# Scores three key tiles ahead of the values, and a new order around them, in a float32 attention block

## The chip, the cores and the metric

The kernel runs on one core of a Trainium2 chip. The metric is the device time of one execution in microseconds. Three runs were timed, and one more execution was profiled.

## The reference

Two residual blocks over `x` of shape (4, 1024, 1024) in float32, cut to what matters:

```python
# block 0
adj = emb_s * emb_t * softmax(x) / sqrt(n)          # diagonal set to -inf
x = x + (1.0 where adj is among the 10240 largest of its 1024 x 1024, else 0)
# block 1: 16 heads of 64
scale, shift = split(cond @ W_emb + b_emb)
xn = rms_norm(x, g_norm) * (1 + scale) + shift
q, k, v = heads(xn @ W_qkv)
q, k = rms_norm(q, g_q), rms_norm(k, g_k)
o = softmax(q @ k.T * d ** -0.5) @ v
x = x + o + o @ W_out
```

## The kernel before

The kernel is written engine by engine: five classes (`Sync`, `Pool`, `Scalar`, `Vector`, `Tensor`) each emit their engine's instructions in a fixed order, and semaphores join them. There is no scheduler; an engine does what comes next in its list, or waits.

Each of the four batches is a loop over eight pairs of heads (`pair`, one method in each class), followed by a `boundary` that projects the outputs and normalises the next batch's features. In a pair `gp` two kinds of work are woven together on TensorE (line 1575 on):

- The attention of pair `gp`. For each head `hh` and each of eight key tiles (128 keys, 1024 queries): `scores` (L1524, four matmuls of 512 columns into two of the four `pst` banks), `exp` on ScalarE (L858 writes the rounded `ph`, L864 the full `pf`), `low` on Pool (L530, `pl = pf - ph`), and `values` (L1544 with `ph` against the values' high and low parts, L1550 with `pl`; accumulated in `ppv`). Over both heads these are 16 tiles, counted `w` within the pair.
- The preparation of pair `gp + 1`, for seven of the eight pairs (`prep`). For each of eight token tiles: `prep_tile` (L1467, three groups of eight matmuls of 384 columns: features high x weights high, high x low, low x high), then ScalarE takes squares, the values' high part and q and k out of `pax` (L825, L828, L835), DVE sums the squares (L1208), scales the sums (L1211) and makes the values' low part (`value_low`, L1218), Pool builds the stacked rows in `stage` (L618 to L636), TensorE transposes them (`transpose_tile`, L1485), and ScalarE copies them out (`stack_tile`, L842 to L844). When all eight are there, `score_max` (L1504, 16 tiles of two matmuls) gives the products of which DVE takes the row maxima (`row_max`, L1225).

Four rules of order matter for the change.

The buffers `ph`, `pf` and `pl` are threefold, so `exp` of tile `w` waits until the values of tile `w - 3` are done. `pst` holds two tiles, so `scores` of tile `w` waits for the exponentials of tile `w - 2`:

```python
e.wait_ge(t_pv, CST + w - 2)      # exp, L856
e.wait_ge(t_ex, CST + w - 1)      # scores, L1521
```

`pax` holds one tile of a preparation, so `prep_tile` of tile `t` waits for the values' low part of tile `t - 1` (semaphore `a_v`). `score_max` of a tile writes the two halves of the other `pax` use, and each half waits for the reduction of the same half of the tile before.

The outputs of pair `gp - 1` are turned at the start of pair `gp`: `out_tokens` (L1560) and `out_rows` (L1572) on TensorE, in two halves, each copied by ScalarE into `ostg` (L877). The transposes of the first prepared tile use the same bank and wait for both copies (`t_oe`).

SyncE issues all DMAs in program order. In a pair it loads the low features of token tiles 0 and 1 (`load_xl`, L348, 512 KB each), then waits for each copied half of the outputs and stores it (L458), and only then loads the low features of tiles 2 to 7. TensorE waits for such a load at the third group of `prep_tile`:

```python
if prep:
    for t in range(2):
        self.load_xl(gp + 1, t)
if not first:
    for h in range(2):
        e.wait_ge(t_oe, 2 * (gp - 1) + h + 1)
        e.dma_start(oT_pairs[...], ostg[...])
if prep:
    for t in range(2, T):
        self.load_xl(gp + 1, t)
```

Beside this, in batches 0 to 2, a search over the next batch's keys for the 10240th largest value runs on DVE in all pairs: counting passes (L1004), and every second tile an update (`search_update`, L1011 to L1016) behind a sum by TensorE (L1477) and a copy by ScalarE (L816). In batch 0, five of the pairs that follow the first, and the first itself, also split the weights of a later pair into high and low parts (L705 on ScalarE, L523 on Pool).

The slots: in steps 8 to 15 the table `slots` says which `score_max` tiles stand before the values, inside them (before their last matmul) and behind them.

Of the kernel before, what the change touches and what calls it, by code (L numbers as in the profile page):

```python
# [48 lines left out]
def cond_block(nc, x, s_in, cond, w_emb, b_emb, g_norm, w_qkv, g_q, g_k, w_out, out, ctx):  # L49
    B, N, D = x.shape  # L50
    T = N // P
# [48 lines left out]
    ahead = sb("ahead", [P, 2, 3], I32)  # L100
# [385 lines left out]
    class Pool:  # L486
# [156 lines left out]
        def pair(self, b, i, par, search, prep, first):  # L643
            e, gp = self.e, PAIRS * b + i
# [26 lines left out]
            for t in range(2, T):  # L671
                if prep:
                    self.prep_tile(gp + 1, t, 1 - par, False)
                self.low(gp, (t + 1) // T, (t + 1) % T)
# [11 lines left out]
    class Scalar:  # L686
# [192 lines left out]
        def pair(self, b, i, par, search, prep, first):  # L879
# [15 lines left out]
            self.exp(gp, 0, 2, new)  # L895
            if not first:
                self.out_rows(gp - 1, 1)
            if prep:
                self.prep_tile(gp + 1, 1 - par, 1)
            self.exp(gp, 0, 3)  # L900
# [4 lines left out]
            for t in range(2, T - 1):  # L905
                if prep:
                    self.prep_tile(gp + 1, 1 - par, t + 1, z=before[t + 1])
                    if t < T - 2:
                        self.stack_tile(gp + 1, 1 - par, t)
                self.exp(gp, (t + 2) // T, (t + 2) % T)  # L910
                if search and not prep and t == 2:
                    self.search_tot(z)
            if prep:
                self.stack_tile(gp + 1, 1 - par, T - 2)
# [5 lines left out]
            self.exp(gp, 1, 1)  # L920
# [18 lines left out]
    class Vector:  # L939
# [304 lines left out]
        def pair(self, b, i, par, search, prep, first):  # L1244
# [11 lines left out]
            for t in range(T):  # L1256
                if prep:
                    self.prep_sums(gp + 1, t)
                if t > 0 and before[t] is not None:
                    self.search_update(before[t])  # L1260
                if prep:
                    self.value_low(gp + 1, 1 - par, t)
# [18 lines left out]
    class Tensor:  # L1281
# [293 lines left out]
        def pair(self, b, i, par, search, prep, first):  # L1575
# [4 lines left out]
            def fill(what):  # L1580
# [3 lines left out]
                elif what is not None:  # L1584
                    self.score_max(gp + 1, 1 - par, what)

            slots = {8: [None, 0, 1], 9: [2, 3, None], 10: [4, 5, None], 11: [6, 7, None], 12: [8, 9, None],
                     13: [10, 11, None], 14: [12, 13, "row"], 15: [14, 15, None]} if prep else {}
# [24 lines left out]
            for t in range(2 * T):  # L1613
                gap = slots.get(t, [None] * 3)
                if t + 2 < 2 * T and not (prep and t == 1):
                    self.scores(gp, par, (t + 2) // T, (t + 2) % T)
# [4 lines left out]
                if prep and t == 0:  # L1621
                    self.prep_tile(gp + 1, 1)
                    self.scores(gp, par, 0, 3)
# [5 lines left out]
                if prep and t == 1:  # L1629
                    self.transpose_tile(gp + 1, 1)  # L1630
                if prep and 1 <= t <= T - 3:
                    self.prep_tile(gp + 1, t + 2, z=before[t + 2])
                    self.transpose_tile(gp + 1, t + 1)
# [74 lines left out]
```

## Time and profile before

| | |
|---|---|
| median of 3 runs | 3757.48 us |
| lowest and highest run | 3756.02 and 3767.08 us |
| the profiled execution | 3765.85 us, of which the profile's span is 3763.9 us |
| TensorE (PE) busy | 3484.9 us, 93% of the span |
| DVE busy | 2480.7 us, 66% |
| ScalarE (ACT) busy | 2027.0 us, 54% |
| Pool busy | 2480.0 us, 66% |
| mean granted TensorE clock | 0.973 of full |

PE stands for TensorE's matmuls, PEld for its weight loads, SPq for SyncE's queue of DMA issues. In rows of the timeline the columns are: start, duration, engine, line, operation, output and inputs by the program's names, shapes, and how many instructions were merged; in brackets the idle time ahead of the row and what ended it. Matmuls overlap by some 0.17 us and their ends are modelled, so the distance from start to start is the better measure. A granted clock of 1.00 is the 2.4 GHz level, 0.50 the 1.2 GHz level. Two views of waits are used: who waited for whom, with the idle time summed, the number of waits and the longest; and the busy time of every engine in a given stretch.

### The profile page before, as it was taken

The numbers are of one execution on the slowest core, as the hardware profiler recorded it, in microseconds if no ns is written. First come the engines' busy times: TensorE is split into PE (matmuls) and PEld (weight loads), VectorE is DVE, ScalarE is ACT, GpSimd is POOL, SyncE is SP. The second block draws the span as 40 slices with busy tenths as digits, with TensorE's granted clock in tenths as the row PEclk, the third lists the DMA queues.
The fourth block names the chain that finished last, engine by engine and source line by source line (L and its number), as shares of the span: only waits on it lengthen the run. The fifth ranks groups of instructions, "written<-read, shape, count | busy, mean of one in ns | idle before, by whom it ended". The sixth has DMA issues, their size and how long they took to land.

```text
span 3763.9 us, 46982 instructions
## 1 busy us (share of the span) xinstructions
PE 3484.9 (93%) x16661; PEld 2542.8 (68%) x16672; DVE 2480.7 (66%) x4056; ACT 2027.0 (54%) x3331; POOL 2480.0 (66%) x2583
## 2 busy tenths in 40 slices
PE   4847999999999999999999999999999999999999
PEld 1225777777756677777756677777755677777754
DVE  8995777777787777777787677777777333333321
ACT  4635555555546355655545455555554455555650
POOL 2027778777646677777756677777765577777750
PEclk9966999999999999999999999999999999999999
DMA  7033223232245222222237222222235322222222
GB/s 291 1 101 112 93 98 105 99 105 101 95 154 193 95 87 99 102 96 84 73 111 235 90 85 89 85 85 88 101 110 172 112 88 87 90 84 91 77 86 94
DMA packets 163305, 399.51 MB, mean 106 GB/s; under 512 B 11848, under 2 KB 83584, under 8 KB 153216
## 3 DMA queue, kind: packets, MB, share of 16 engines
q1 hardware_dynamic: 163072, 396.52, 29.8%
q8 instruction: 133, 2.18, 0.2%
q14 instruction: 100, 0.82, 0.1%
HBM read 302.10 MB, written 94.37 MB: 105 GB/s over the span
## 4 chain that ended last, share of the span: by engine, by line
PE 69%; DVE 13%; POOL 10%; ACT 4%; DMA 2%; issue 2%; SPq 0%; POOLq 0%; DVEq 0%; ACTq 0%
PE pax L1467 26%; PE pst L1524 9%; PE ppv L1544 9%; PE pst L1440 8%; PE pax L1504 5%; PE ppv L1550 4%; POOL pl L530 3%; DVE mx L1225 3%; PE pst L1304 2%; PE pax L1485 2%; DMA xl<-xl_scr 2%; POOL xlo L554 1%; DVE xr L1056 1%; POOL wl L523 1%; POOL rs L618 1%
## 5 line engine op out<-in xcount | busy, mean ns | idle before, releaser
L530 POOL TENSOR_TENSOR pl<-pf,ph 128x1024 fp32r<-128x1024 f32 x512 | 1219.6, 2392 | 203.1 <-ACT pf L864 200.8
L1004 DVE TENSOR_SCALAR_CACHE_REDUCE trash<-keys,state 128x2048 uint8<-128x2048 f32 x384 | 899.2, 2342 | 7.7
L1225 DVE TENSOR_REDUCE mx<-pax 128x1 f32<-128x512 f32 x960 | 618.2, 686 | 271.2 <-PE pax L1504 270.5
L858 ACT ACTIVATE ph<-pst 128x1024 fp32r<-128x1024 f32 x512 | 523.1, 1022 | 223.3 <-PE pst L1524 215.5
L864 ACT ACTIVATE pf<-pst 128x1024 f32<-128x1024 f32 x512 | 522.7, 1021 | 0.4 <-DMA out_x<-pf 0.4
L1208 DVE TENSOR_REDUCE ss<-sq 128x4 f32<-128x256 f32 x256 | 107.3, 419 | 609.3 <-ACT sq L825 609.3
L618 POOL TENSOR_TENSOR rs<-rs,half 128x4 f32<-128x4 f32 x256 | 265.2, 1036 | 292.9 <-DVE rs L1211 288.9
L1467 PE MATMUL pax<-wh,xh 128*128 128x384 f32 x1920 | 394.2, 348 | 46.1 <-DVE vl L1218 39.8
L1467 PEld LDWEIGHTS pax<-wh,xh 128*128 128x128 f32 x1920 | 339.0, 192 | 81.4 <-DVE vl L1218 55.7
L1467 PE MATMUL pax<-wl,xh 128*128 128x384 f32 x1920 | 385.1, 339 | 0.0
L1504 PE MATMUL pax<-sA 65*128 65x512 f32 x960 | 351.7, 433 | 33.8 <-DVE mx L1225 17.5
L1550 PE MATMUL ppv<-pl,vh 128*65 128x512 f32 x1024 | 360.1, 397 | 7.9 <-POOL pl L530 7.9
L1467 PE MATMUL pax<-wh,xl 128*128 128x384 f32 x1792 | 356.5, 342 | 10.6 <-DMA xl<-xl_scr 10.6
L1524 PE MATMUL pst<-sA 65*128 65x512 f32 x1024 | 343.5, 417 | 5.0 <-ACT sA L849 4.4
L1467 PEld LDWEIGHTS pax<-wl,xh 128*128 128x128 f32 x1920 | 338.6, 190 | 0.0
L1467 PEld LDWEIGHTS pax<-wh,xl 128*128 128x128 f32 x1792 | 321.1, 190 | 12.6 <-DMA xl<-xl_scr 12.6
L825 ACT ACTIVATE sq<-pax 128x256 f32<-128x256 f32 x240 | 91.2, 380 | 437.5 <-PE pax L1467 437.3
L1524 PE MATMUL pst<-sB 128*128 128x512 f32 x1024 | 326.0, 400 | 0.0
L1544 PE MATMUL ppv<-ph,vh 128*65 128x512 f32 x1024 | 322.0, 396 | 0.9 <-issue 0.5
L1544 PE MATMUL ppv<-ph,vl 128*65 128x512 f32 x1024 | 319.9, 393 | 0.0
L1504 PEld LDWEIGHTS pax<-sA 65*128 65x128 f32 x960 | 179.9, 190 | 177.9 <-DVE mx L1225 131.6
L546 POOL TENSOR_SCALAR rsx<-ssx 128x1 f32<-128x1 f32 x32 | 22.6, 706 | 325.6 <-ACT otok L728 324.3
(198 smaller groups left out, 5625.7 us busy)
## 6 DMA issues: line engine op xcount, KB each, us to landing
xl<-xl_scr SPq DMA_DIRECT2D x224, 512.0 KB, 3.3
wh<-w_scr SPq DMA_DIRECT2D x24, 1536.0 KB, 6.2
wl<-w_scr SPq DMA_DIRECT2D x24, 1536.0 KB, 9.6
keys<-in_x SPq DMA_DIRECT2D x32, 512.0 KB, 5.3
xl_scr<-xlo SPq DMA_DIRECT2D x64, 256.0 KB, 3.2
wo<-wo_scr SPq DMA_DIRECT2D x4, 4096.0 KB, 13.6
pf<-out_x SPq DMA_DIRECT2D x64, 256.0 KB, 3.8
out_x<-pf SPq DMA_DIRECT2D x64, 256.0 KB, 3.1
```

Source lines behind the costliest of these rows:

```text
L530: e.tensor_tensor(pl[:, w % 3, :], pf[:, w % 3, :], ph[:, w % 3, :].bitcast(F32), ALU.subtract).then_inc(t_lo, 1)
L618: e.tensor_tensor(rs[:, cols], rs[:, cols], half4[:], ALU.pow).then_inc(a_rs, 1)
L858: e.activation(ph[:, w % 3, :], src, ACT.Exp, scale=DH ** -0.5).then_inc(t_eh, 1)
L864: e.activation(pf[:, w % 3, :], src, ACT.Exp, scale=DH ** -0.5).then_inc(t_ex, 1)
L1004: e.tensor_scalar(trash[:], kv, thr_f, None, ALU.is_ge, ALU.add, accum_out=cnt[:, c:c + 1]).then_inc(z_cnt, 1)
L1225: e.tensor_reduce(mx2[:, j // T, j % T, c:c + 1], max_banks(alone, j)[:, c, :], axis=AX, op=ALU.max).then_inc(m_mx, 1)
L1440: i = e.matmul(pst[:, q % 4, :], heads_of(b, k, t), wo[b % 2][:, k, c * HALF:(c + 1) * HALF], start=(k == 0), stop=(k == KT - 1), skip_gro ...
L1467: i = e.matmul(qkv_bank(alone, t)[:, 0:6 * DH], a, w[:, k, :, :].rearrange("p s c -> p (s c)"), start=(n == 0), stop=(n == 3 * KT - 1), sk ...
L1504: e.matmul(max_banks(alone, j)[:, c, :], sA[par][0:DH + 1, hh, qt * P:(qt + 1) * P], sA[par][0:DH + 1, 2 + hh, c * HALF:(c + 1) * HALF], s ...
L1524: i = e.matmul(pst[:, 2 * (kt % 2) + c, :], op[0:k, 2 + hh, kt * P:(kt + 1) * P], op[0:k, hh, c * HALF:(c + 1) * HALF], start=(m == 0), st ...
L1544: e.matmul(ppv[0:DH + 1, c, :], v[:, par, kt, hh, :], ph[:, w % 3, c * HALF:(c + 1) * HALF], start=(kt == 0 and m == 0), stop=False, skip_ ...
L1550: i = e.matmul(ppv[0:DH + 1, c, :], vh[:, par, kt, hh, :], pl[:, w % 3, c * HALF:(c + 1) * HALF], start=False, stop=(kt == T - 1), skip_gr ...
```

## The change

On TensorE, in pairs with preparation: the scores run three tiles ahead of the values instead of two; in step 0 the preparation of tile 1 and the scores of tile 3 stand ahead of the values of tile 0; in steps 1 to 6 the transposes of tile `t` and then the scores of tile `t + 3` stand ahead of the values; the slots of the score maxima are dealt out anew. On ScalarE the exponentials of a step stand ahead of that step's copies, and in step 0 the copy of the second half of the output rows stands behind the exponentials of tile 3. On Pool the low part stands ahead of a tile's stage. On DVE the values' low part stands ahead of the search update. Last pairs of a batch, without preparation, keep their order. SyncE's order is unchanged.

```diff
@@ Pool.pair
             for t in range(2, T):
+                self.low(gp, (t + 1) // T, (t + 1) % T)
                 if prep:
                     self.prep_tile(gp + 1, t, 1 - par, False)
-                self.low(gp, (t + 1) // T, (t + 1) % T)
@@ Scalar.pair
             self.exp(gp, 0, 2, new)
+            if prep:
+                self.prep_tile(gp + 1, 1 - par, 1)
+                self.exp(gp, 0, 3)
             if not first:
                 self.out_rows(gp - 1, 1)
-            if prep:
-                self.prep_tile(gp + 1, 1 - par, 1)
-            self.exp(gp, 0, 3)
+            if not prep:
+                self.exp(gp, 0, 3)
...
             for t in range(2, T - 1):
+                self.exp(gp, (t + 2) // T, (t + 2) % T)
                 if prep:
                     self.prep_tile(gp + 1, 1 - par, t + 1, z=before[t + 1])
-                    if t < T - 2:
-                        self.stack_tile(gp + 1, 1 - par, t)
-                self.exp(gp, (t + 2) // T, (t + 2) % T)
+                    self.stack_tile(gp + 1, 1 - par, t)
...
             if prep:
-                self.stack_tile(gp + 1, 1 - par, T - 2)
+                self.exp(gp, 1, 1)
             self.out_move(gp, 0, (PAIRS - 1) * b + i)
...
             if prep:
                 self.stack_tile(gp + 1, 1 - par, T - 1)
-            self.exp(gp, 1, 1)
+            else:
+                self.exp(gp, 1, 1)
@@ Vector.pair
                 if prep:
                     self.prep_sums(gp + 1, t)
+                if prep:
+                    self.value_low(gp + 1, 1 - par, t)
                 if t > 0 and before[t] is not None:
                     self.search_update(before[t])
-                if prep:
-                    self.value_low(gp + 1, 1 - par, t)
@@ Tensor.pair
-            slots = {8: [None, 0, 1], 9: [2, 3, None], 10: [4, 5, None], 11: [6, 7, None], 12: [8, 9, None],
-                     13: [10, 11, None], 14: [12, 13, "row"], 15: [14, 15, None]} if prep else {}
+            slots = {8: [None, 0, 1], 9: [2, 3, None], 10: [4, 5, 6], 11: [7, 8, None], 12: [9, 10, None],
+                     13: [11, 12, None], 14: [13, 14, "row"], 15: [15, None, None]} if prep else {}
+            ahead = 3 if prep else 2
...
             for t in range(2 * T):
                 gap = slots.get(t, [None] * 3)
-                if t + 2 < 2 * T and not (prep and t == 1):
-                    self.scores(gp, par, (t + 2) // T, (t + 2) % T)
+                if prep and t == 0:
+                    self.scores(gp, par, 0, 2)
+                    self.prep_tile(gp + 1, 1)
+                if prep and 0 < t < T - 1:
+                    self.transpose_tile(gp + 1, t)
+                if t + ahead < 2 * T:
+                    self.scores(gp, par, (t + ahead) // T, (t + ahead) % T)
                 fill(gap[0])
                 self.values(gp, par, t // T, t % T, lambda: fill(gap[1]))
                 if t == 0 and not first:
                     self.out_rows(gp - 1, 1)
                 if prep and t == 0:
-                    self.prep_tile(gp + 1, 1)
-                    self.scores(gp, par, 0, 3)
                     self.prep_tile(gp + 1, 2, hi=8)
...
-                if prep and t == 1:
-                    self.transpose_tile(gp + 1, 1)
                 if prep and 1 <= t <= T - 3:
                     self.prep_tile(gp + 1, t + 2, z=before[t + 2])
-                    self.transpose_tile(gp + 1, t + 1)
```

TensorE at the start of a pair with outputs to write, before, from the scores of tile 2 (`pst<-sA`, `pst<-sB`) to the first group of the preparation of tile 2 (`otok` are the output rows, `wh,xh` begins a preparation):

```order
L1524 MATMUL pst<-sA 128x512 x2
L1524 MATMUL pst<-sB 128x512 x2
L1544 MATMUL ppv<-ph,vh 65x512 x2
L1544 MATMUL ppv<-ph,vl 65x512 x2
L1550 MATMUL ppv<-pl,vh 65x512 x2
L1572 MATMUL pax<-identr,otok 128x128 x4
L1467 MATMUL pax<-wh,xh 128x384 x8
L1467 MATMUL pax<-wl,xh 128x384 x8
L1467 MATMUL pax<-wh,xl 128x384 x8
```

The same place after the change, as far as the first group of the preparation of tile 2:

```order
L1526 MATMUL pst<-sA 128x512 x2
L1526 MATMUL pst<-sB 128x512 x2
L1469 MATMUL pax<-wh,xh 128x384 x8
L1469 MATMUL pax<-wl,xh 128x384 x8
L1469 MATMUL pax<-wh,xl 128x384 x8
L1526 MATMUL pst<-sA 128x512 x2
L1526 MATMUL pst<-sB 128x512 x2
L1546 MATMUL ppv<-ph,vh 65x512 x2
L1546 MATMUL ppv<-ph,vl 65x512 x2
L1552 MATMUL ppv<-pl,vh 65x512 x2
L1574 MATMUL pax<-identr,otok 128x128 x4
L1469 MATMUL pax<-wh,xh 128x384 x8
```

The values of tile 0 and the output rows behind them have moved behind a whole preparation and the scores of tile 3. (Lines are two higher in the changed file.)

ScalarE at the same place, before, from the first half of the output rows (`ostg`) to the exponentials of tile 3:

```order
L877 ACTIVATE ostg<-pax 128x512
L858 ACTIVATE ph<-pst 128x1024
L864 ACTIVATE pf<-pst 128x1024
L877 ACTIVATE ostg<-pax 128x512
L825 ACTIVATE sq<-pax 128x256
L828 ACTIVATE vh<-pax 128x2x64
L835 ACTIVATE qkn<-pax 128x256
L858 ACTIVATE ph<-pst 128x1024
L864 ACTIVATE pf<-pst 128x1024
```

And after:

```order
L877 ACTIVATE ostg<-pax 128x512
L858 ACTIVATE ph<-pst 128x1024
L864 ACTIVATE pf<-pst 128x1024
L825 ACTIVATE sq<-pax 128x256
L828 ACTIVATE vh<-pax 128x2x64
L835 ACTIVATE qkn<-pax 128x256
L858 ACTIVATE ph<-pst 128x1024
L864 ACTIVATE pf<-pst 128x1024
L877 ACTIVATE ostg<-pax 128x512
```

The second copy of output rows has moved behind the copies of preparation 1 and the exponentials of tile 3.

TensorE in step 10, after the change, from score maximum 4 (`pax<-sA`) to the scores of the next step:

```order
L1506 MATMUL pax<-sA 128x512 x2
L1546 MATMUL ppv<-ph,vh 65x512 x2
L1546 MATMUL ppv<-ph,vl 65x512 x2
L1552 MATMUL ppv<-pl,vh 65x512
L1506 MATMUL pax<-sA 128x512 x2
L1552 MATMUL ppv<-pl,vh 65x512
L1506 MATMUL pax<-sA 128x512 x2
L1526 MATMUL pst<-sA 128x512 x2
```

Before, the last `pax<-sA` row of these wasn't there; the scores followed the one matmul on `pl` at once.

## Rows read from the trace of the kernel before

**Rows 1.** Busy time by stretch, of three pairs: us, engines' busy (instructions), clock, DMA.

```profile
core 0: us, PE busy (x) PEld busy (x) DVE busy (x) ACT busy (x) POOL busy (x), PEclk, DMA share, GB/s
752.50:845.60 93.10, 88.16 (x465) 69.73 (x465) 69.03 (x112) 55.33 (x98) 74.47 (x77) 1.00 0.30 102
1444.10:1534.40 90.30, 87.48 (x465) 69.92 (x465) 69.06 (x112) 52.64 (x95) 67.54 (x74) 1.00 0.24 88
3158.00:3246.60 88.60, 86.44 (x457) 69.03 (x457) 29.97 (x64) 51.98 (x87) 67.49 (x74) 1.00 0.24 90
```

**Rows 2.** Waits of PE, 1444 to 1534 us (three rows) and 3158 to 3246 us (last).

```profile
PE pax L1467 <- DVE vl L1218: 1.5, 2, 0.9
PE pax L1504 <- DVE mx L1225: 0.6, 2, 0.3
PE pax L1485 <- POOL stage L636: 0.2, 1, 0.2
...
PE pax L1467 <- DVE vl L1218: 0.9, 1, 0.9
```

**Rows 3.** Timeline of PE, 1451 to 1468 us.

```profile
1452.45 0.63 PE L1544 MATMUL ppv<-ph,vh 128*65 128x512 f32 x2
...
1453.83 0.60 PE L1572 MATMUL pax<-identr,otok 128*128 128x128 f32 x4
...
1454.19 1.64 PE L1467 MATMUL pax<-wh,xh 128*128 128x384 f32 x8
...
1458.46 0.64 PE L1524 MATMUL pst<-sA 65*128 65x512 f32 x2
...
1460.43 1.66 PE L1467 MATMUL pax<-wh,xh 128*128 128x384 f32 x8 [0.87 <-DVE vl L1218]
...
1463.69 1.57 PE L1467 MATMUL pax<-wh,xl 128*128 128x384 f32 x8
...
1466.73 0.46 PE L1485 MATMUL pax<-identr,stage 128*128 128x128 f32 x4
...
1467.83 1.66 PE L1467 MATMUL pax<-wh,xh 128*128 128x384 f32 x8 [0.64 <-DVE vl L1218]
```

**Rows 4.** Timeline of ACT, exponentials 2, second output rows, exponentials 3.

```profile
1454.48 1.06 ACT L864 ACTIVATE pf<-pst 128x1024 f32<-128x1024 f32 x1
...
1455.38 0.65 ACT L877 ACTIVATE ostg<-pax 128x512 f32<-128x512 f32 x1
...
1459.60 1.02 ACT L858 ACTIVATE ph<-pst 128x1024 fp32r<-128x1024 f32 x1
...
1460.52 1.03 ACT L864 ACTIVATE pf<-pst 128x1024 f32<-128x1024 f32 x1
```

**Rows 5.** SyncE's issues, then landings of L348: tile 2 alone, and 1450 to 1475.

```profile
1453.73 2.64 SPq L458 DMA_DIRECT2D oT_scr<-ostg  x2
1456.41 16.23 SPq L348 DMA_DIRECT2D xl<-xl_scr  x4
...
DMA to landing us min/median/max: 3.7/3.7/3.7
...
DMA to landing us min/median/max: 3.2/3.5/4.3
```

**Rows 6.** Timeline of POOL and DVE, 1455 to 1464 us.

```profile
1455.42 4.74 POOL L530 TENSOR_TENSOR pl<-pf,ph 128x1024 fp32r<-128x1024 f32 x2
...
1459.61 0.58 DVE L1211 TENSOR_SCALAR rs<-ss 128x4 f32<-128x4 f32 x1
...
1460.30 2.33 DVE L1004 TENSOR_SCALAR_CACHE_REDUCE trash<-keys,state 128x2048 uint8<-128x2048 f32 x1
...
1463.73 0.46 POOL L636 TENSOR_TENSOR stage<-qkn,stage 128x128 fp32r<-128x128 f32 x1
...
1466.66 0.17 DVE L1211 TENSOR_SCALAR rs<-ss 128x4 f32<-128x4 f32 x1
```

**Rows 7.** Timeline of PE and DVE at score maxima 0 and 1.

```profile
1508.05 0.63 PE L1504 MATMUL pax<-sA 65*128 65x512 f32 x2
1508.51 0.40 PE L1550 MATMUL ppv<-pl,vh 128*65 128x512 f32 x1
1509.22 1.10 PE L1504 MATMUL pax<-sA 65*128 65x512 f32 x2 [0.31 <-DVE mx L1225]
1510.16 0.62 PE L1524 MATMUL pst<-sA 65*128 65x512 f32 x2
...
1508.47 2.57 DVE L1225 TENSOR_REDUCE mx<-pax 128x1 f32<-128x512 f32 x4 [2.28 <-PE pax L1504]
```

**Rows 8.** First pair of batch 1: PE's wait, and 3.4 us behind it.

```profile
PE pax L1467 <- DVE vl L1218: 2.4, 2, 1.8
...
1279.00:1282.40 3.40, 3.40 (x15) 3.30 (x14) 3.36 (x3) 0.99 (x3) 2.20 (x6) 0.50 0.00 0
```

**Rows 9.** Waits of PE, a pair of batch 0, 752 to 845 us.

```profile
PE pax L1467 <- DMA xl<-xl_scr: 1.7, 1, 1.7
...
PE ppv L1550 <- POOL pl L530: 0.5, 2, 0.2
```

**Rows 10.** The 3.4 us behind two waits for a load, batch 0.

```profile
571.40:574.80 3.40, 3.40 (x19) 3.09 (x20) 1.26 (x4) 1.69 (x4) 0.59 (x1) 1.00 0.14 52
...
664.60:668.00 3.40, 3.40 (x10) 3.30 (x11) 0.07 (x1) 0.49 (x3) 0.00 (x0) 0.50 0.14 52
```

## The prediction, made before the changed kernel had run

> **What bounds the kernel.** I cut the trace into pairs first. A pair of heads that also prepares the next pair takes 93.1 us in batch 0, 90.3 in batches 1 and 2, 88.6 in batch 3, TensorE is busy for all but 2 to 5 us of it, and its granted clock is 1.00 [rows 1]. There are 28 such pairs, seven in each batch, and the change touches them alone. So TensorE's own order bounds them, and only what lengthens or shortens its waits counts. I measure a wait from the start of one group to the start of the next, less what the group takes elsewhere, since the ends of matmuls are modelled.
>
> The waits of one pair, by who ended them, are in [rows 2]: two on the low part of the values, two on the row maxima, one on Pool's stage. The timeline [rows 3] places the first two. Scores of tile 3 start at 1458.46 and take 0.93, but the preparation of tile 2 starts at 1460.43: 1.0 us lost. The preparation of tile 3 starts at 1467.83, 1.1 after four transposes that take 0.3: 0.8 lost. Batch 3 has the first alone (last row) [rows 2].
>
> **The change, part by part.** One preparation is 4.2 us, one scores group 0.93, one values group 1.4 (1452.45 to 1453.83, with its output rows 0.36 more) [rows 3]. No work is added; order decides everything.
>
> *Second wait.* Scores of tile 4 now stand between the preparations of tiles 2 and 3, 0.93 us of cover against a wait of 0.8, and the value's low part no longer stands behind the search update. It goes: -0.8 in the 18 pairs with search that are not a batch's first, **-14**. What is late next there is Pool's stage of tile 1, ready at 1464.2 (1463.73 + 0.46) [rows 6], some 2 us before it is asked for.
>
> *Output rows and what hangs on them.* This is the part that the words of the change don't name. Values 0 move behind preparation 1 and scores 3; ScalarE now does exponentials 3 ahead of the second half of the output rows. Exponentials of tile w wait for values w - 3, because they reuse the buffer. So on the old clock: preparation 1 starts at 1452.45 instead of 1454.19, ends 1456.65; scores 3 to 1457.6; values 0 to 1458.95, drained at 1459.15. Exponentials 3 take 1.95 (1459.60 to 1461.55) [rows 4]: to 1461.1. The copy of the output rows ends 0.5 after the exponential ahead of it (1455.54 and 1456.03) [rows 4]: at 1461.6. The old time was 1456.03. Behind this copy wait, in SyncE's queue, the second store of the rows and then the load of the low features for tile 2 [rows 5]: it was issued 0.4 after the copy and landed 3.7 later. Now it is issued at 1462.0 and lands at 1465.7. TensorE needs it for the third group of preparation 2, which started at 1463.69 [rows 3]. By then the same matmuls have been issued in both orders, so the difference is the whole cost: **+2.0 us**. The first wait (1.0) and the transposes of tile 0, which wait for the same copy, lie inside that path and cost nothing on top. The 24 pairs that have output rows to write: 24 x 2.0 = **+48**. Bounds: the load may land in 3.2 or 4.3 (the shortest and longest of the four around there [rows 5]), so 1.5 to 2.6 each.
>
> *Score maxima.* Scores now end one step earlier, and the table of slots puts maximum 6 right behind 5, and 11 right behind 10, with one 0.24 us matmul between. The trace shows such a neighbourhood: maximum 0 starts at 1508.05, and with maximum 1 the two take to 1510.16, 2.11 us, where their five matmuls need 0.46 + 0.24 + 0.46 = 1.16. The price is 0.95, for DVE needs 2.57 for four reductions [rows 7]. Before, this happens at 0-1 and 11-12 in full, and at 13-14 with the output of the row maxima between (0.46). After, the full ones are 0-1, 5-6, 10-11 and 12-13, and 14-15 has the rows between. Two more: 2 x 0.95 x 28 = **+53**. Bounds: DVE is idle for part of each step, so a later one could be cheaper, 0.5; more than 0.95 it can't be without an earlier debt, which the scores between pay off.
>
> *First pair of a batch.* It has no output rows, so the +2.0 is absent. Its two waits show 2.4 us idle, the longer 1.8 [rows 8], and after the longer one the granted clock is 0.50 for 3.4 us. Afterwards Pool's stage for tile 1 (second subtraction, then 4 us) is the latest and keeps about 1 us. Gain 3 each, four pairs: **-12**.
>
> *Batch 0.* Pool also splits weights in five of these pairs, works without a break at the end and makes values wait; the low-feature load of tile 0 comes 1.7 late behind it [rows 9]. With exponentials a step earlier Pool starts this row of work some 2 us earlier: about -1 each, **-5**; the ends are 0 and -2.
>
> *Clock.* The new wait for the load leaves TensorE idle for about 2 us in one piece. The trace has two waits on such a load of 1.7 us idle each, almost alike: after the one that ended at 571.3 the granted clock stayed 1.00, with 19 matmuls in 3.4 us; after the one that ended at 664.5 it was 0.50 (the 1.2 GHz level) with 10 in 3.4 us [rows 10]. Nine of nineteen lost is 1.6 us. Which of the two a pair meets the trace doesn't tell; I take half of 24: 12 x 1.6 = **+19**, ends 0 and +38.
>
> *Update behind the low part.* The search's small DVE operations come 0.3 later, and the counting passes behind them (2.33 each [rows 6], two a step) fill 4.7 of the 7 us of a step (4.2 + 0.93 + 1.4 and the transposes); nobody waits for them: 0.
>
> *Steps 3 to 7.* ScalarE, Pool and TensorE keep their spacing (Pool has 2.4 for a subtraction and 4 for a stage, 6.4 us of work in 7.0); 0, and the 0.3 on Pool's last stage stays.
>
> **Sum:** 48 - 14 + 53 - 12 - 5 + 19 = **+89**. It is made on the profiled execution of 3765.85 us (span 3763.9), which is 8.4 above the median of the three runs, 3757.48. The waits are the same in both, so I put the 89 on the median: **3846**.
>
> **A rule beside a row.** The small scaling of the squares' sums on DVE takes 0.17 as a rule, and 0.58 at 1459.61, where it ends at 1460.19, within 0.03 of Pool's second subtraction (1455.42 + 4.74) [rows 6]. So the first wait comes from Pool holding DVE, and moving values behind the preparation doesn't by itself end it: the scaling would now be issued at about 1457.8, inside the same two subtractions. It matters for the second rival below. The Trainium skill, GPSIMD Engine Reference, section Specifications, says that GpSimd shares its SBUF interfaces with VectorE, with contention for VectorE instructions in a two-port mode or with two SBUF inputs; by that rule the first wait stays wherever the long subtractions lie beside the scaling, and the trace agrees. By it the second rival comes out at 3779 and not at 3755.
>
> **The rivals.**
> 1. *The forecast*, 0.64: both new waits. Its own range: no clock loss at all, short landings and cheaper maxima give 3757 + 36 - 14 + 28 - 12 - 5 = 3790; all clocks lost, long landings and nothing gained in batch 0 give 3757 + 62 - 14 + 53 - 12 + 38 = 3884.
> 2. *The load isn't late, only the maxima cost*, 0.16. It needs the copy of the output rows before about 1459.6, that is exponentials 3 not held by values 0. Against it speaks the wait in the code. The first wait stays as it is, since Pool holds DVE in the same way. 53 - 14 - 12 - 5 = +22: 3779. Were the first wait to vanish too, 24 less, 3755, no difference.
> 3. *Faster*, 0.09. Mechanism: the extra neighbours among the maxima are free, because DVE has only 32 reductions of 0.64 us (21 us) for the 25 us that the maxima take, and the load is in time. The old waits then go: 28 x 1.0 + 21 x 0.8, with the first pairs' clock (4 x 1.6) and batch 0's 5: -56, 3701. It decides at the step from maximum 5 to 6: if it takes 1.16 rather than 2.11 us. Against it: the reductions can't begin before their maximum is there, as at 0-1.
> 4. *No net change*, 0.05: maxima at half price and the load late by less than its cover.
> 5. *More than the range*, 0.06: a debt that grows through steps 3 to 7, such as Pool's stage late at every tile, 0.5 us in six steps of 28 pairs, +84 more: 3930.
>
> A measurement of this kernel can tell about 0.3% (11 us) from no change. Slower by more: 0.86, cases 1, 2 and 5. Same: 0.05. Faster: 0.09. The range has to leave out no more than 0.2: I take 3775 to 3878, which holds the forecast without its last corner, and case 2.
>
> **What would show it.** Right: in a pair with output rows TensorE waits for the load of low features some 2 us at tile 2; that load is issued at about 18 us from the pair's first output transposes instead of 12.3; four full stalls of 0.95 among the maxima instead of two; the pairs of batches 1 and 2 take 93 to 95 us instead of 90.3, those of batch 3 some 92.5 to 94; the wait at tile 3 is gone; short stretches at clock 0.50. Wrong: pairs at 92 us with no wait on the load (case 2), or below 90 (case 3).

## The result and the profile after

| | before | after |
|---|---|---|
| median, 6 runs each on the same chips | 3763.35 us | 3873.16 us (3862.23 to 3876.79) |
| ratio | | 1.029, 95% interval 1.027 to 1.031 |
| the profiled execution | 3765.85 us, span 3763.9 | 3874.18 us, span 3872.3 |
| TensorE (PE) busy | 3484.9 us | 3537.6 us |
| mean granted clock | 0.973 | 0.964 |

The changed kernel is slower by 110 us (3873.16 - 3763.35); 89 had been forecast. In the changed file TensorE's and DVE's lines are two higher than before.

Waits of PE over the whole span of the changed kernel (who waited for whom: us in total, times, longest):

```profile
PE pax L1469 <- DMA xl<-xl_scr: 62.5, 24, 3.6
...
PE pax L1506 <- DVE mx L1227: 34.8, 112, 0.3
PE pax L1487 <- POOL stage L636: 28.0, 42, 4.5
PE pax L1469 <- DVE vl L1220: 19.3, 23, 0.9
```

The same view of the kernel before:

```profile
PE pax L1467 <- DVE vl L1218: 39.8, 49, 1.8
...
PE pax L1485 <- POOL stage L636: 24.4, 37, 4.5
...
PE pax L1504 <- DVE mx L1225: 17.5, 56, 0.3
PE pax L1467 <- DMA xl<-xl_scr: 10.6, 6, 2.1
```

Three lines moved most. The low-feature load, formerly waited for in 6 places, is waited for in 24: the pairs with output rows to write. The maxima stall 4 times a pair instead of 2 (112 and 56 over 28 pairs). The value's low part is waited for 23 times instead of 49. What remains there is the first wait. Pool's stage is waited for a little longer, 28.0 us instead of 24.4.

A pair whose clock stayed at 1.00, and the 3.4 us behind two of the new waits (us, busy by engine, clock, DMA):

```profile
2253.60:2347.80 94.20, 88.48 (x465) 70.21 (x465) 70.86 (x112) 53.02 (x95) 67.50 (x74) 1.00 0.23 84
...
2276.10:2279.50 3.40, 3.40 (x20) 3.04 (x21) 0.84 (x4) 1.51 (x7) 0.18 (x1) 1.00 0.30 95
1480.10:1483.50 3.40, 2.93 (x10) 2.93 (x11) 0.00 (x0) 0.00 (x0) 0.07 (x1) 0.50 0.02 10
```

The pair takes 94.2 us where [rows 1] had 90.3; other pairs of batches 1 and 2 run to 99.0, and the difference is mostly the clock. The last line shows it: it begins 0.47 us before its wait ends, at 1480.57, and its 10 matmuls run in the 2.93 us behind that, at clock 0.50. From here on, time at clock 0.50 is added up over the 24 pairs that have output rows to write, each from its first output transpose to that of the pair behind it: 13.7 us before, all of it in batch 0, and 105.8 in the changed kernel. I now go through this pair, which starts at 2253.6. TensorE:

```profile
2267.09 0.63 PE L1546 MATMUL ppv<-ph,vh 128*65 128x512 f32 x2
...
2269.93 1.66 PE L1469 MATMUL pax<-wh,xh 128*128 128x384 f32 x8 [0.86 <-DVE vl L1220]
2271.43 0.46 PE L1487 MATMUL pax<-identr,stage 128*128 128x128 f32 x4
2271.72 1.63 PE L1469 MATMUL pax<-wl,xh 128*128 128x384 f32 x8
2276.09 1.68 PE L1469 MATMUL pax<-wh,xl 128*128 128x384 f32 x8 [2.74 <-DMA xl<-xl_scr]
...
2280.50 0.69 PE L1469 MATMUL pax<-wh,xh 128*128 128x384 f32 x3
```

The third group of preparation 2 starts 22.5 us into the pair; in [rows 3] it started at 19.6 (1463.69 - 1444.10). So 2.9 us are lost; over all 24 pairs the group starts 2.8 later in the mean, if 19.6 is taken for batch 0 too. Preparation 3 starts at 2280.50, with no bracket: the second wait has gone. ScalarE and SyncE's queue show what the load hung on:

```profile
2268.74 1.02 ACT L858 ACTIVATE ph<-pst 128x1024 fp32r<-128x1024 f32 x1 [1.56 <-PE ppv L1552]
2269.66 1.02 ACT L864 ACTIVATE pf<-pst 128x1024 f32<-128x1024 f32 x1
2270.56 0.61 ACT L877 ACTIVATE ostg<-pax 128x512 f32<-128x512 f32 x1
...
2263.23 8.28 SPq L458 DMA_DIRECT2D oT_scr<-ostg  x2
2271.55 6.57 SPq L348 DMA_DIRECT2D xl<-xl_scr  x3
```

Exponentials 3 wait for values 0, the copy of the rows stands behind them, and the load leaves at 2271.55, 17.95 into the pair (12.3 before, [rows 5]). It landed 4.5 us later.

### The profile page after: what moved, and what is told of

The parts are those of the page before. It is cut to its first block, busy times and chain, and to the rows that moved or that the text cites. A ratio compares the mean times of both kernels' runs of the same rounds, so it can differ in the third digit from the quotient of the medians.

```text
span 3872.3 us, 46982 instructions
## 1 busy us (share of the span) xinstructions
PE 3537.6 (91%) x16661; PEld 2577.6 (67%) x16672; DVE 2522.6 (65%) x4056; ACT 2038.1 (53%) x3331; POOL 2478.7 (64%) x2583
## 4 chain that ended last, share of the span: by engine, by line
PE 68%; DVE 12%; POOL 9%; ACT 4%; DMA 3%; issue 2%; SPq 0%; POOLq 0%; DVEq 0%; ACTq 0%
PE pax L1469 23%; PE ppv L1546 10%; PE pst L1526 10%; PE pst L1442 7%; DVE mx L1227 5%; PE pax L1506 5%; PE ppv L1552 4%; DMA xl<-xl_scr 3%; PE pst L1306 2%; PE pax L1487 2%; POOL xlo L554 2%; POOL rs L618 1%; DVE xr L1058 1%; POOL pl L530 1%; POOL qkn L621 1%
## 5 line engine op out<-in xcount | busy, mean ns | idle before, releaser
L1469 PE MATMUL pax<-wh,xl 128*128 128x384 f32 x1792 | 370.6, 351 | 62.5 <-DMA xl<-xl_scr 62.5
L1506 PE MATMUL pax<-sA 65*128 65x512 f32 x960 | 370.3, 443 | 56.6 <-DVE mx L1227 34.8
L1469 PEld LDWEIGHTS pax<-wh,xh 128*128 128x128 f32 x1920 | 348.2, 194 | 58.9 <-DVE vl L1220 24.8
L1469 PEld LDWEIGHTS pax<-wh,xl 128*128 128x128 f32 x1792 | 329.2, 195 | 70.3 <-DMA xl<-xl_scr 70.2
L825 ACT ACTIVATE sq<-pax 128x256 f32<-128x256 f32 x240 | 91.2, 380 | 320.4 <-PE pax L1469 320.2
L1526 PEld LDWEIGHTS pst<-sB 128*128 128x128 f32 x1024 | 199.5, 195 | 46.9
```

Of the source, the lines that this page charges most:

```text
L1469: i = e.matmul(qkv_bank(alone, t)[:, 0:6 * DH], a, w[:, k, :, :].rearrange("p s c -> p (s c)"), start=(n == 0), stop=(n == 3 * KT - 1), sk ...
L1506: e.matmul(max_banks(alone, j)[:, c, :], sA[par][0:DH + 1, hh, qt * P:(qt + 1) * P], sA[par][0:DH + 1, 2 + hh, c * HALF:(c + 1) * HALF], s ...
L1526: i = e.matmul(pst[:, 2 * (kt % 2) + c, :], op[0:k, 2 + hh, kt * P:(kt + 1) * P], op[0:k, hh, c * HALF:(c + 1) * HALF], start=(m == 0), st ...
```

## The experiments

Each was timed beside the kernel before on the same chips (whose medians there are 3763.8 to 3765.8 us); ratios are to that, with the 95% interval.

**The load taken out of its queue place.** SyncE issues the load of tile 2 between the two stores.

```diff
                     e.dma_start(oT_pairs[...], ostg[...])
+                    if prep and h == 0:
+                        self.load_xl(gp + 1, 2)
             if prep:
-                for t in range(2, T):
+                for t in range(2 if first else 3, T):
```

> The changed kernel, but SyncE issues the load of the low features of tile 2 between the two stores of output rows instead of behind both. Theory 1 (the load waits in SyncE's queue behind a copy that waits for values 0): the load is issued about 10 us into a pair and lands before 15, TensorE's wait of about 3 us at the third group of preparation 2 is gone, and with it most of the short stretches at clock 0.50 behind it: 24 x 2.9 = 70 less and 25 to 30 for the clock, so 3770 to 3785. The first wait of 1.0 at preparation 2 stays. Theory 2 (the new order itself, a preparation without values between, is what costs; the load only happens to end it): another wait takes its place at the same group or the transposes ahead of it, and the time stays above 3840.

Measured 3765.14 us, ratio 1.0006 (0.9996 to 1.0015). One DMA in another place takes back 108 of the 110 us. TensorE waits for no load of low features any more, and pairs take 91.2 us in batches 0 to 2 alike. It came out below the expected span because two more things went with the stall: the 105.8 us at clock 0.50 fall to nothing, and batch 0, whose pairs took 93.1 to 94.8 before, waits no more for the load of tile 0.

**The old slots under the new order.** The table of slots put back, the rest as changed.

```diff
-            slots = {8: [None, 0, 1], 9: [2, 3, None], 10: [4, 5, 6], 11: [7, 8, None], ...
+            slots = {8: [None, 0, 1], 9: [2, 3, None], 10: [4, 5, None], 11: [6, 7, None], ...
```

> The changed kernel with the old table of slots for the score maxima (4,5 / 6,7 / ... / 14,15), scores still three ahead. Theory 1: neighbouring maxima cost 0.95 us each; there are three full ones a pair (0-1, 9-10, 11-12) instead of four, so 28 x 0.95 = 27 less: about 3846. Theory 2 (the maxima are free, DVE has time enough): no difference, 3873.

Measured 3856.08 us, 1.025 (1.0232 to 1.0268): 17 less than the changed kernel, where one stall of 0.95 in 28 pairs makes 27. The stalls did fall as they should:

```profile
PE pax L1506 <- DVE mx L1227: 26.3, 84, 0.3
```

84 is three a pair, as expected. The profiled executions differ by 22.7 us (3874.18 and 3851.45), the medians by 17. Of the other 4 to 10 us the trace shows 4: it has 30 waits for the low-feature load instead of 24, and the six more, all for tile 0 in batch 0, come to 4.0 us. The rest isn't settled; both kernels lose an amount to the clock that changes from run to run (four runs of this one lie between 3851.45 and 3861.92).

**Both together.**

> Both: the load of tile 2 between the stores, and the old slots. Theory 1: the two are apart in time and add, 3873 - 97 - 27 = about 3749, somewhat below the kernel before (3763). Theory 2: 3840 or more.

Measured 3743.76 us, 0.9948 (0.9932 to 0.9964). With the load early, the old slots are worth 21 us (3765.14 - 3743.76). So the order of the change, without its late load and one of its two extra stalls, is faster than the kernel before.

**The new slots alone, in the kernel before.**

> The kernel before with the new table of slots alone. Theory 1: neighbours are then 0-1, 5-6 and 12-13 in full, and 14-15 with the rows between; one more than before, 28 x 0.95 = 27 more, about 3790. Theory 2 (maxima free): no difference.

Measured 3787.57 us, 1.0062 (1.0049 to 1.0075). With scores two ahead, the scores still lie between maxima 10 and 11, so one stall is added, not two. The stretch of one pair:

```profile
1445.70:1536.90 91.20, 88.00 (x464) 69.79 (x464) 69.02 (x112) 52.60 (x95) 67.63 (x74) 1.00 0.24 87
```

The waits on the maxima over the whole span, three a pair:

```profile
PE pax L1504 <- DVE mx L1225: 25.5, 84, 0.3
```

A pair takes 91.2 instead of 90.3: 0.92 for one neighbourhood, in the mean of the 18 such pairs of batches 1 to 3, against the 0.95 read off [rows 7]. In batch 0 the pairs grow by 0.3 only, since waits for Pool's low part get shorter beside it.

**The copy of the rows ahead of exponentials 3.** In the changed kernel, on ScalarE.

```diff
             if prep:
                 self.prep_tile(gp + 1, 1 - par, 1)
-                self.exp(gp, 0, 3)
             if not first:
                 self.out_rows(gp - 1, 1)
-            if not prep:
-                self.exp(gp, 0, 3)
+            self.exp(gp, 0, 3)
```

> The changed kernel, but ScalarE copies the second half of the output rows ahead of exponentials 3 (where TensorE has them ready at about 15.4 us into the pair). Theory 1: the copy ends 1.6 us earlier, the load is issued 1.6 earlier, and a wait of about 1.3 instead of 3 us is left at the third group of preparation 2: 24 x 1.6 = 38 less and some of the clock, 3815 to 3835. Theory 2: nothing, or the wait of the exponentials moves elsewhere: above 3860.

Measured 3800.09 us, 1.0093 (1.0077 to 1.0109): 73 less, where 38 and some of the clock were expected, so it fell below the expected span. The wait shrank as it should, by 33 us in all (62.5 to 29.6). What was underrated is the clock: of the 105.8 us at 0.50 only 6.8 are left. Less is saved than by moving the load itself, since the rows are turned behind values 0 and the copy can't come before that. What is left of the wait:

```profile
PE pax L1467 <- DMA xl<-xl_scr: 29.6, 24, 2.9
```

**The landing.** The forecast had the load land in 3.7 us; here it took 4.5, and the load of tile 3 was issued directly behind it. In the changed kernel SyncE now holds that load until tile 2's has landed.

```diff
                 for t in range(2, T):
+                    if t == 3:
+                        e.wait_ge(d_xl[0], 16 * (T * (gp - b) // 2 + 2))
                     self.load_xl(gp + 1, t)
```

> The changed kernel, with SyncE waiting until the load for tile 2 has landed before it issues the one for tile 3. It asks why the wait for the load was 2.9 us longer than the old start of that group and not 2.0. Theory 1: in the changed order the load for tile 3 is ready to go at once behind that for tile 2 and shares the DMA engines with it, so that tile 2 lands in 4.5 (3.8 to 5.3) instead of 3.7; held back, tile 2 lands in 3.7 again, every one of 24 waits is 0.8 shorter, 19 less, and perhaps some of the clock: 3840 to 3855. Theory 2 (the landing is longer for another cause, such as the search's or stores' traffic): the landing stays at 4.5 and the time within 5 of 3873.

Measured 3861.11 us, 1.0259 (1.0243 to 1.0275), 12 less than the changed kernel and 6 above the expected span. In the trace the tile 2 load's median landing over the 24 pairs went from 4.4 (3.7 to 5.3) back to 3.8, and the 24 waits from 2.6 us to 2.1 in the mean, 0.5 each where 0.8 was expected. In the pair that starts at 2241.2 the third group stands 21.65 in:

```profile
2262.85 2.87 PE L1471 MATMUL pax<-wh,xl 128*128 128x384 f32 x8 [1.91 <-DMA xl<-xl_scr]
```

That is 2.05 later than before, against the 2.0 of the forecast; over all 24 pairs it is 2.3 instead of 2.8. So the chain was priced rightly, and most of the rest was the second load close behind. Two pairs still had landings of 4.8 and 5.1 us, which nothing here explains. (Its profiled execution took 3844.84 us, the least of its four, with 54.6 us at clock 0.50.)

**The value's low part ahead of the update, alone.** In the kernel before, on DVE.

```diff
+                if prep:
+                    self.value_low(gp + 1, 1 - par, t)
                 if t > 0 and before[t] is not None:
                     self.search_update(before[t])
-                if prep:
-                    self.value_low(gp + 1, 1 - par, t)
```

> The kernel before with one part of the change alone: on DVE the values' low part stands ahead of the search update. Theory 1: the wait of 0.8 at preparation 3 comes from the update (0.7 us of small operations) that the low part stood behind; it goes in the 21 pairs with search: 21 x 0.7 = 15 less, 0.4%. Theory 2 (the wait belongs to the chain square, sum, low part, which is too long whatever the update does): under 4 less.

Measured 3748.70 us, 0.9959 (0.9946 to 0.9973). It removes the whole second wait. A pair takes 89.6 us:

```profile
1436.10:1525.70 89.60, 87.44 (x464) 69.93 (x464) 69.10 (x113) 52.69 (x95) 67.73 (x74) 1.00 0.25 89
```

And PE's waits for the value's low part in it, one where [rows 2] has two:

```profile
PE pax L1467 <- DVE vl L1218: 0.8, 1, 0.8
```

**Pool's subtraction 2 behind the stage of tile 1, alone.** In the kernel before. This part is not in the change: it tests why the first wait is there.

```diff
             self.low(gp, 0, 1)
-            self.low(gp, 0, 2)
             if prep:
                 self.prep_tile(gp + 1, 1, 1 - par, False)
+            self.low(gp, 0, 2)
```

> The kernel before, but on Pool the low part of exponential tile 2 stands behind the stage of token tile 1 instead of ahead of it, so that no long Pool subtraction runs while DVE wants to scale the squares' sums. Theory 1 (Pool holds DVE): the scaling takes 0.17 and not 0.58 (1.48 in first pairs), the values' low part ends 0.4 earlier, and the wait of 1.0 at preparation 2 shrinks to about 0.6; in first pairs it goes from 1.9 to 0.5 and the stretch at clock 0.50 with it: 24 x 0.4 + 4 x 3 = 22 less. Theory 2 (the length of the scaling is its own): no difference there.

Measured 3743.58 us, 0.9947 (0.9934 to 0.9959). At this place DVE's scaling no longer lies beside a subtraction, and the first wait falls from 1.0 to 0.6 (the scores of tile 3 start at 1451.04 and take 0.93):

```profile
1452.18 0.17 DVE L1211 TENSOR_SCALAR rs<-ss 128x4 f32<-128x4 f32 x1
...
1452.60 1.66 PE L1467 MATMUL pax<-wh,xh 128*128 128x384 f32 x8 [0.46 <-DVE vl L1218]
```

The 24 pairs behind a batch's first give 12 of the profiled execution's 22 us, the stretches from a batch's last pair to the next one's second 11.

**The last two together.**

> The two edits of the kernel before together: the values' low part ahead of the update on DVE, low part 2 behind the stage of tile 1 on Pool. Theory 1: they add, 15 + 22 = 37 less, 3726, faster than both kernels by 1%. Theory 2: under 5 less.

Measured 3730.06 us, 0.9908 (0.9895 to 0.9922). The two are separate: 15.6 and 20.7 alone make 36, and 34 are there.

**Four parts mended in the changed kernel.** Load ahead, old slots, rows before exponentials 3, and Pool's subtraction 2 behind stage 1; the scores stay three ahead.

> The changed kernel with four edits: load of tile 2 between the stores, old slots, output rows ahead of exponentials 3 on ScalarE, and low part 2 behind the stage of tile 1 on Pool. Theory 1: against the kernel with the first two (3744) the first wait of 1.0 goes, since nothing long is on Pool when DVE scales, and the transposes of tile 0 no longer wait for the copy: 24 x 1.0 and a little in first pairs, 3710 to 3722, below the 3730 of the kernel before with two orders changed. Theory 2 (the first wait is a chain of its own length): 3740.

Measured 3743.14 us, 0.9947 (0.9935 to 0.996): a miss by at least 20. The first wait and the load's wait are gone, but there is a new one at tile 3. TensorE, DVE and Pool in the pair that starts at 1423.0:

```profile
1446.74 1.65 PE L1469 MATMUL pax<-wh,xh 128*128 128x384 f32 x8 [0.77 <-DVE vl L1220]
...
1444.39 2.11 DVE L1213 TENSOR_SCALAR rs<-ss 128x4 f32<-128x4 f32 x1
...
1441.73 4.74 POOL L532 TENSOR_TENSOR pl<-pf,ph 128x1024 fp32r<-128x1024 f32 x2
```

The change puts Pool's subtraction 3 ahead of the stage of tile 2. With subtraction 2 moved behind the stage of tile 1 the two adjoin: 4.74 us without a gap, to 1446.47. DVE's scaling of tile 2 is issued into them and ends at 1446.50. The wait has moved one tile on.

**Maxima spread evenly.** The kernel with the last two orders, with each inner maximum ahead of the fourth of the six matmuls of `values`, and the first eight maxima dealt anew.

```diff
                 for c in range(2):
+                    if m and c and between is not None:
+                        between()
...
-            slots = {8: [None, 0, 1], 9: [2, 3, None], 10: [4, 5, None], 11: [6, 7, None], ...
+            slots = {8: [None, None, 0], 9: [1, 2, None], 10: [3, 4, None], 11: [5, 6, 7], ...
```

> The kernel before with the two orders changed (3730), and the maxima dealt out evenly: the one inside the values stands after three of their six matmuls instead of after five, step 8 has one, steps 9 to 15 two, step 11 three. Theory 1 (a neighbour costs because DVE needs 1.3 us for its two reductions and TensorE comes back after 0.7): starts are then never closer than 1.16, about five stalls of 0.13 are left instead of 0.95 + 0.95 + 0.46, 1.7 less in 28 pairs, 48 in all: about 3682. Theory 2 (the price is that of switching between maxima and values): no gain, or a loss, 3730 or more.

Measured 3769.69 us, 1.0012 (1.0003 to 1.0021): 40 above its base, where a gain was expected. PE, then DVE, at three maxima:

```profile
1499.01 0.63 PE L1504 MATMUL pax<-sA 65*128 65x512 f32 x2
1500.19 1.10 PE L1504 MATMUL pax<-sA 65*128 65x512 f32 x2
1501.12 0.40 PE L1546 MATMUL ppv<-ph,vl 128*65 128x512 f32 x1
1501.36 0.63 PE L1550 MATMUL ppv<-pl,vh 128*65 128x512 f32 x2
...
1499.44 2.58 DVE L1225 TENSOR_REDUCE mx<-pax 128x1 f32<-128x512 f32 x4 [0.87 <-PE pax L1504]
```

Three matmuls between two maxima put them 1.18 apart, and the second then takes 0.93 instead of 0.47 (from its start to that of the matmul behind it). Its second half needs the bank that DVE releases 0.43 + 1.29 us after the first maximum's start. With five matmuls between, as in the old slots, they are 1.63 apart and nothing is lost (the changed kernel, 2323.53 and 2325.16; DVE idles 0.32 between them):

```profile
2323.53 0.63 PE L1506 MATMUL pax<-sA 65*128 65x512 f32 x2
...
2325.16 0.66 PE L1506 MATMUL pax<-sA 65*128 65x512 f32 x2
...
2325.59 1.29 DVE L1227 TENSOR_REDUCE mx<-pax 128x1 f32<-128x512 f32 x2 [0.32 <-PE pax L1506]
```

So an even deal made nearly every second maximum stall in order to save the few that did. A new wait came with it: with one maximum less in step 8, the scores behind it wait 0.5 us for the exponentials, 31 waits and 14.0 us in the whole trace, where the kernel before has 3 and 0.6.

**Values 0 behind preparation 1, with the scores two ahead.** The kernel with the last two orders, the load between the stores, and TensorE's step 0 as in the change. On ScalarE the copies of preparation 1 now stand ahead of the second copy of output rows, and exponentials 3 stay behind it. The diff below shows TensorE alone.

```diff
+                if prep and t == 0:
+                    self.prep_tile(gp + 1, 1)
+                    self.scores(gp, par, 0, 3)
                 fill(gap[0])
                 self.values(...)
                 if t == 0 and not first:
                     self.out_rows(gp - 1, 1)
                 if prep and t == 0:
-                    self.prep_tile(gp + 1, 1)
-                    self.scores(gp, par, 0, 3)
                     self.prep_tile(gp + 1, 2, hi=8)
```

> The kernel before, with the two orders that each gained (the update behind v's low part on VectorE, the low features of tile 2 behind the staging of tile 1 on GpSimd, together 3730), the load of tile 2's low features between the two stores, and on TensorE the preparation of tile 1 and the scores of tile 3 ahead of the values of tile 0; the scores stay two key tiles ahead and keep their old slots, ScalarE copies the output rows ahead of the exponentials of tile 3. Theory 1 (what is left of the first wait, 0.62 in each of 24 pairs and more in the first ones, stands only because TensorE comes to the preparation of tile 1 with nothing in front that could be done): about 3714 (3708 to 3720), faster than both kernels, pairs of about 88.5. GpSimd's subtractions for tiles 2 and 3 should not run back to back as they did with four parts changed, so VectorE's scaling isn't held. Theory 2 (a later values 0 makes the output rows and the load late as in the changed kernel, or VectorE is held and a new wait stands at tile 2 or 3): 3730 or more.

Measured 3709.26 us, 0.986 (0.9841 to 0.9879): faster than both kernels, by 55 and by 164 us. TensorE, DVE and Pool at the same place:

```profile
1440.81 0.60 PE L1574 MATMUL pax<-identr,otok 128*128 128x128 f32 x4
1441.17 1.64 PE L1469 MATMUL pax<-wh,xh 128*128 128x384 f32 x8
...
1447.28 0.17 DVE L1213 TENSOR_SCALAR rs<-ss 128x4 f32<-128x4 f32 x1
...
1437.26 2.38 POOL L532 TENSOR_TENSOR pl<-pf,ph 128x1024 fp32r<-128x1024 f32 x1
...
1444.62 2.40 POOL L532 TENSOR_TENSOR pl<-pf,ph 128x1024 fp32r<-128x1024 f32 x1
```

The stretch of this pair:

```profile
1425.90:1514.30 88.40, 87.10 (x465) 70.11 (x465) 68.75 (x112) 52.59 (x95) 67.64 (x74) 1.00 0.25 90
```

Values and output rows fill what was the first wait, Pool's subtractions lie apart, and the pair takes 88.4 us. Of [rows 2] only the maxima (0.6) and Pool's stage (0.2) are left.

## Why the prediction was right, and where its sizes were off

The sign and the mechanism hold: 3873 lies in the range, and the two new waits stand where they were put. It lies 5 us below the range's upper end. Of the 27 us between 3846 and 3873, 6 are the kernel before, whose median was 3757.48 in the three runs that the forecast had and 3763.35 in six. By its own steps, against the difference of the two spans, 108.4 us:

| term | forecast | found | from |
|---|---|---|---|
| second wait | -14 | -14 | gone in the trace; alone -15.6 |
| output rows and the load | +48 | +66 | 24 pairs, 2.8 in the mean |
| score maxima | +53 | +52 | 56 more stalls; 0.92 for each, measured alone |
| first pairs of a batch | -12 | -17 | start of the span to batch 0's second pair, and from each batch's last pair to the next one's second: -1.5, -2.9, -4.6, -0.2, together -9, and the 7 that their own maxima cost are in the line above |
| batch 0 | -5 | -17 | six pairs: shortest 94.3 instead of 93.1 + 4.0 |
| clock | +19 | +38 | what remains of 108.4; not measured by itself |

Load and clock cost 37 us more than forecast, and the first pairs and batch 0 gained 17 more than forecast. That the sum is off by only 19 is in part luck: errors of both signs met in it. (Part of the first pairs' gain is clock too: those stretches have 17 us less at 0.50.)

**Output rows.** The chain was foretold link by link: the load issued 17.9 into the pair (found 17.95), exponentials 3 held by values 0. The step that was mis-sized is "landed 3.7 later". A single load had shown that figure [rows 5]; here it landed in 4.5 (4.4 in the median of the 24 pairs), and tile 3's load was issued right behind it. With that load held back the loss was 2.05 in one pair and 2.3 in the mean. The bound of the forecast, 2.6, was too low, for it was taken from landings around and not from a pair of loads issued together.

**Score maxima.** Right in size and place. The changed kernel alone shows the count of four; the price comes from the slots alone, 0.92 for one more in a pair (+23.3 over all 28, batch 0 giving some of it back).

**Second and first wait.** The second went, and its cause is the update: one exchange on DVE does it without anything else of the change. The first stayed, as forecast, and the row beside the rule was the right one to look at. In the changed kernel the scaling comes just before the seam between Pool's subtractions 1 and 2, misses it, and is held through the whole second one:

```profile
2264.93 4.73 POOL L530 TENSOR_TENSOR pl<-pf,ph 128x1024 fp32r<-128x1024 f32 x2
...
2267.29 2.40 DVE L1213 TENSOR_SCALAR rs<-ss 128x4 f32<-128x4 f32 x1
2269.60 0.28 DVE L1220 TENSOR_TENSOR vl<-pax,vh 128x128 fp32r<-128x128 f32 x1
2269.80 2.33 DVE L1006 TENSOR_SCALAR_CACHE_REDUCE trash<-keys,state 128x2048 uint8<-128x2048 f32 x1
```

Before, it came later in the second subtraction and lost 0.4; now 2264.93 + 4.73 is 2269.66, and the scaling, due at 2267.46, ends at 2269.69. The wait at tile 2 is no longer than it was, since TensorE also comes there later. The Trainium skill, GPSIMD Engine Reference, section Specifications, names a contention between the two engines for some of VectorE's instructions, and the trace agrees, with 2.40 us against 0.17.

**Batch 0.** The forecast gave 1 us a pair to Pool's earlier start. It left out that SyncE's load of the next pair's tile 0, for which TensorE waited 1.7 at a pair's start [rows 9], would be waited for no more: the 10.6 us in 6 waits of before are gone. In the kernel with the load between the stores, batch 0's pairs are as short as the others.

**Clock.** "I take half of 24: 12 x 1.6" is the other step that was mis-sized. In 18 of the 24 pairs the clock fell, and for 5.9 us each in the mean (105.8 / 18). Of the 92.1 us more than before at 0.50, at most half is lost, 46 us, which leaves room for the 38 of the table. The trace of before could have said more than the two waits that were weighed: it has six for such a load, in batch 0, and four of them, those that ended at 476.9, 664.5, 852.1 and 946.6, were followed by a clock of 0.50. With the load early no such time is left in the 24 pairs. Moving it gave back 108 us, 4.5 in each: 2.8 of wait and 1.7 beside it, which the clock can cover (at most 105.8 / 2 / 24 = 2.2).

**The rivals.** The second (the load in time, only the maxima cost) can be built, by moving the one DMA: 1 us above the kernel before rather than its 22. Most of the difference is batch 0, whose six pairs behind the first got 16 us shorter in all (563.5 to 547.4) in spite of two more stalls each. It fell by the wait of exponentials 3 on values 0, as argued. The third (free neighbours) falls with the slots alone. The fifth, a growing debt, isn't there: pairs of batches 1 and 2 with an undisturbed clock take 94.2, the 90.3 of before with the terms above.

## What to carry to other kernels

When a group moves back in one engine's order, follow what is queued behind its readers to the end, through the in-order queue of DMA issues, and compare the arrival with the need: here one load in the wrong place cost more than all the rest of the change, and moving that alone gave it back. Run the parts of a change one by one in both kernels: the value's low part ahead of the update was worth 15.6 us by itself, TensorE's step 0 with the load in time 21 more, and both were hidden under the rest. The trace may offer what the change doesn't, here Pool's subtraction 2 behind the stage of tile 1, 20.7 us. And look at which long operations an order puts side by side on a third engine: two adjoining subtractions on Pool held a DVE instruction of 0.17 us, and with it TensorE, at one tile or another, until they were kept apart (3743 with three tiles ahead, 3709 with two; those two kernels differ in Pool's and ScalarE's order as well, so the lead by itself isn't priced).

## What the runs showed of the hardware that was not expected

- DVE's scaling of 128 x 4 elements takes 0.17 us and up to 2.40 beside Pool's subtractions: it ends when the subtraction under way ends, and one issued at the seam of two waits for the whole second. This holds throughout: in the traces of the kernel before and of the changed one, all 47 scalings that were issued more than 0.15 us before the end of a subtraction end 0.02 to 0.03 us behind it, and in the changed kernel 23 that were issued within 0.05 us of that end took 2.36 to 2.40. DVE's reduction of 0.42 us at 2266.76, inside the first subtraction, and its counting pass of 2.35 at 2263.45, half a microsecond and more of it beside the same one, weren't lengthened. So only some forms are held. Which property of a form decides isn't tested here.
- A load of 512 KB that landed in 3.7 us alone took 4.5 with a second one issued directly behind it, and 3.7 again with that one held (medians over 24 pairs: 4.4 and 3.8).
- Of two waits for a load of much the same kind, one (3.01 us idle, ended 1480.57) was followed by a clock of 0.50 and 10 matmuls in 2.93 us, the other (2.74, ended 2276.09) by 1.00 and 20 in 3.4 us. Over all 24 waits of the changed kernel, 1.9 to 3.6 us long, the clock fell behind 18, and it stayed up behind one of 3.2 (ended 3543.4). With the rows ahead of exponentials 3 it stayed up behind 22 of 24 waits, 0.5 to 2.1 us long, and fell behind the other two, of 1.8 and 2.9. So shorter waits cost it less often, but the length alone doesn't tell them apart; what does stays open.
